# Whole vector operations in the recurrent scan, with TensorE's output and value products spread over the steps of a group

## The reference

```python
q, k = x @ W_q.T, x @ W_k.T          # per head
v = x @ W_v.T
b = (q * k).sum(-1) * SCALE
alpha = x @ W_alpha_w.T + W_alpha_b
a = -softplus(alpha).sum(-1)
vs, vl = sign(v), log(abs(v) + EPS)
def step(carry, inp):                # 64 steps, one after another
    ln, nm, sg = carry
    ln = stable_lse(a_t + ln, b_t)
    dec = a_t[..., None] + nm
    new = b_t[..., None] + vl_t[:, None, :]
    m = maximum(dec, new)
    ssum = sg * exp(dec - m) + vs_t * exp(new - m)
    nsg = sign(ssum)                 # 1 where 0
    nm = m + log(abs(ssum) + EPS)
    y = (nsg * exp(nm - ln[..., None])).sum(-2)
    return (ln, nm, nsg), y
y @ W_o.T
```

## Time and profile before

| what | value |
|---|---|
| median of 3 runs | 2039.79 us |
| profiled execution | 2044.84 us, its span 2042.4 us |
| mean granted TensorE clock | 0.943 of full speed |
| PE, DVE, ACT busy, share of the span | 92%, 65%, 55% |
| the scan's loop, first `s` to last new state | 1542.69 to 1811.08 us, 268.4 us |

### The profile page before, as it was taken

One profiled execution on the slowest core, in us unless ns is written; L12 is line 12 of the kernel. 1 busy time (PEld: TensorE's weight loads), 2 busy tenths in 40 slices (PEclk: granted clock), 3 DMA queues, 4 the chain that ended last, 5 costly groups with the idle time before them and its releaser, 6 DMA issues. The chain is left out here.

```text
span 2042.4 us, 31431 instructions
## 1 busy us (share of the span) xinstructions
PE 1881.7 (92%) x10506; PEld 1501.4 (74%) x10506; DVE 1333.6 (65%) x2451; ACT 1124.4 (55%) x1864; POOL 136.6 (7%) x130
## 2 busy tenths in 40 slices
PE   7989985999997599999999999999968899889998
PEld 4667875999996578787878787878746667665664
DVE  4784546999996474636363545454528898878686
ACT  5762324888885354545454444444426666656663
POOL 0001000111110110000000000000000000002221
PEclk9999976999999799999999999999987988879999
DMA  6300042453424221101010101012040000020000
GB/s 235 108 32 1 1 161 90 150 205 128 178 89 165 93 71 34 51 16 51 15 51 15 51 15 51 15 51 82 16 141 42 1 1 1 1 88 1 1 21 21
DMA packets 22750, 129.80 MB, mean 64 GB/s; under 512 B 3601, under 2 KB 3857, under 8 KB 18962
## 3 DMA queue, kind: packets, MB, share of 16 engines
q1 hardware_dynamic: 17714, 112.59, 15.0%
q0 software_dynamic: 4960, 16.26, 2.4%
HBM read 116.51 MB, written 12.32 MB: 63 GB/s over the span
## 5 line engine op out<-in xcount | busy, mean ns | idle before, releaser
L116 PE MATMUL PS<-cT,qs 128*128 128x512 f32 x1152 | 298.4, 404 | 3.3 <-DVE qs L1697 2.2
L116 PE MATMUL PS<-pT,cN 128*128 128x512 f32 x1152 | 269.8, 392 | 1.7 <-DVE pT L1697 1.7
L116 PEld LDWEIGHTS PS<-cT,qs 128*128 128x128 f32 x1152 | 209.5, 188 | 52.6 <-issue 8.9
L116 PEld LDWEIGHTS PS<-pT,cN 128*128 128x128 f32 x1152 | 213.9, 188 | 45.0 <-DVE pT L1697 1.9
L116 PE MATMUL PS<-fw,xgT 128*128 128x384 f32 x1104 | 204.6, 340 | 5.7 <-DVE xgT L1244 5.7
L116 PEld LDWEIGHTS PS<-fw,xgT 128*128 128x128 f32 x1104 | 193.3, 190 | 9.3 <-DVE xgT L1244 6.3
L1692 DVE TENSOR_REDUCE nmax<-PS 128x1 f32<-128x512 f32 x128 | 87.8, 686 | 156.5 <-PE PS L116 156.4
L1244 DVE TENSOR_TENSOR fw<-W,fw 128x1536 fp32r<-128x1536 f32 x92 | 159.4, 1755 | 22.8 <-ACT fw L1164 22.8
L116 PE MATMUL PS<-xT,ws 128*128 128x512 f32 x576 | 155.1, 422 | 15.1 <-PEq L2599 8.7
L1597 ACT ACTIVATE qp<-PS 128x512 f32<-128x512 f32 x96 | 57.4, 598 | 187.9 <-PE PS L116 187.9
L1164 ACT ACTIVATE fw<-W 128x1536 fp32r x92 | 134.4, 1488 | 33.2 <-issue 33.2
(11 more groups left out here) (289 smaller groups left out, 3406.8 us busy)
## 6 DMA issues: line engine op xcount, KB each, us to landing
W<-in_fc SPq DMA_DIRECT2D x8, 3072.0 KB, 11.0
cT<-in_ctxT SPq DMA_DIRECT2D x16, 768.0 KB, 4.3
raw_pj<-in_proj SPq DMA_DIRECT2D x8, 1536.0 KB
ct_in<-in_ctxT SPq DMA_DIRECT2D x16, 768.0 KB, 4.3
cn_in<-in_ctxN SPq DMA_DIRECT2D x16, 768.0 KB
W<-in_w SPq DMA_DIRECT2D x2, 4096.0 KB, 13.1
routed_y<-y POOLq DMA_DIRECT2D x22, 256.0 KB
W<-in_w SPq DMA_DIRECT2D x5, 1024.0 KB, 7.1
```

The lines of the kernel that those rows point to most:

```text
L116: mm = nc.tensor.matmul(out, lhs(m, s), rhs(n, s), start=(opens and (s, m, n) == terms[0]), stop=((s, m, n) == terms[-1]))
```

## The change

Three edits of VectorE's program, two of TensorE's, and a PSUM bank.

- `s`, `ep` and `sg` become one operation each of 512 columns. The last one, the new state, stays in halves, with ScalarE's `ear` and TensorE's `head_sums` that read it.
- eal and ebe of a group come from one operation over a tile that holds al and be side by side.
- `out_proj(c - 1)`, four steps of contraction, is spread: two of them at j = 3, one at 4, one at 5. The product for v of group c + 2 is spread: half of its 12 matmuls at j = 6, half at 7.
- The transposes of x use PSUM bank 0 in place of bank 3, so `turn_x` waits for `q_sb` in place of `z_used`, and `out_proj` no longer waits for `xT_ready`.

```diff
+    OUT_AT = {3: range(0, 2), 4: range(2, 3), 5: range(3, DK)}
...
+        coefs, small = sbuf("coefs5", [P, 2, S]), sbuf("small5", [P, 2, S])
+        (al, be), (eal, ebe) = ([tile[:, n, :] for n in range(2)] for tile in (coefs, small))
...
-        ln = Norm(nc, e, "5", sbuf, ps[3], xT[0])
+        ln = Norm(nc, e, "5", sbuf, ps[0], xT[0])
...
-                def project(c, w):
+                def project(c, w, ks=range(DK)):
...
-                    split_product(nc, bank, lambda part, k: xT[c % 2][part][:, k, :],
-                                  lambda part, k: ws[part][:, ORDER.index(w), k, :], DK, w != W5_A).then_inc(done, 1)
+                    n = ORDER.index(w)
+                    for k in ks:
+                        for m, r in ((0, 0), (0, 1), (1, 0)):
+                            mm = nc.tensor.matmul(bank, xT[c % 2][m][:, k, :], ws[r][:, n, k, :],
+                                                  start=(k == 0 and m == r and w != W5_A),
+                                                  stop=(k == DK - 1 and m == 1))
+                    if ks[-1] == DK - 1:
+                        mm.then_inc(done, 1)
...
-                    pe.wait_ge(ln.xT_ready, BASE + min(c + 4, NG))
...
-                    pe.wait_ge(z_used, BASE + max(c - 3, 0))
+                    pe.wait_ge(q_sb, BASE + c)
                     ln.tensor(pe, c)
...
-                        elif j == 5 and c >= 1:
-                            out_proj(c - 1)
+                        elif j == 6 and c + 2 < NG:
+                            project(c + 2, W5_V, range(0, 2))
                         elif j == 7 and c + 2 < NG:
-                            project(c + 2, W5_V)
+                            project(c + 2, W5_V, range(2, DK))
+                        if c >= 1 and j in OUT_AT:
+                            out_proj(c - 1, OUT_AT[j])
                         head_sums(t)
...
-                    ch.link(nc.vector.tensor_scalar(eal[:, now(c)], al[:, now(c)], EPS, None, ALU.mult))
-                    ins = nc.vector.tensor_scalar(ebe[:, now(c)], be[:, now(c)], EPS, None, ALU.mult)
+                    ins = nc.vector.tensor_scalar(small[:, :, now(c)], coefs[:, :, now(c)], EPS, None, ALU.mult)
...
-                        for h, cols in enumerate(HALVES):
-                            ve.wait_ge(r_sb, BASE + 2 * t + h + 1)
-                            nc.vector.scalar_tensor_tensor(s_[:, cols], old[:, cols], al[:, t:t + 1], bv[:, t % 2, cols],
-                                                           ALU.mult, ALU.add).then_inc(s_sb, 1)
+                        ve.wait_ge(r_sb, BASE + 2 * t + 2)
+                        nc.vector.scalar_tensor_tensor(s_[:, :], old, al[:, t:t + 1], bv[:, t % 2, :],
+                                                       ALU.mult, ALU.add).then_inc(s_sb, 2)
...
-                        for h, cols in enumerate(HALVES):
-                            ve.wait_ge(ear_sb, BASE + 2 * t + h + 1)
-                            nc.vector.tensor_tensor(ep[:, cols], ear[:, cols], ebv[:, t % 2, cols],
-                                                    ALU.max).then_inc(ep_sb, 1)
+                        ve.wait_ge(ear_sb, BASE + 2 * t + 2)
+                        nc.vector.tensor_tensor(ep[:, :], ear[:, :], ebv[:, t % 2, :], ALU.max).then_inc(ep_sb, 2)
...
+                        ve.wait_ge(s_sb, BASE + 2 * t + 2)
+                        ve.wait_ge(ep_sb, BASE + 2 * t + 2)
+                        nc.vector.scalar_tensor_tensor(sg[:, :].bitcast(U32), s_[:, :].bitcast(U32), SIGN_BIT,
+                                                       ep[:, :].bitcast(U32), ALU.bitwise_and,
+                                                       ALU.bitwise_or).then_inc(sg_sb, 2)
                         ve.wait_ge(y_mm, BASE + t + 1)
                         for h, cols in enumerate(HALVES):
-                            ve.wait_ge(sg_sb, BASE + 2 * t + h + 1)
+                            ve.wait_ge(sg_sb, BASE + 2 * t + 2)
                             nc.vector.tensor_tensor(new[:, cols], s_[:, cols], sg[:, cols], ALU.add).then_inc(r_sb, 1)
```

More of the change, by code:

```diff
@@ L1832, in decayed_attention_layer @@
         mx, dn = sbuf("mx5", [P, 1 + S]), sbuf("dn5", [P, 1 + S])
-        t1, t2, eA, eB, rd, al, be, eal, ebe = (sbuf(n, [P, S]) for n in ("t15", "t25", "eA5", "eB5", "rd5", "al5", "be5",
-                                                                       "eal5", "ebe5"))
+        t1, t2, eA, eB, rd = (sbuf(n, [P, S]) for n in ("t15", "t25", "eA5", "eB5", "rd5"))
+        coefs, small = sbuf("coefs5", [P, 2, S]), sbuf("small5", [P, 2, S])
+        (al, be), (eal, ebe) = ([tile[:, n, :] for n in range(2)] for tile in (coefs, small))
         bv, ebv = sbuf("bv5", [P, 2, D]), sbuf("ebv5", [P, 2, D])
@@ L1938, in head_sums, with out_proj @@
                     mm.then_inc(y_mm, 1)
-                def out_proj(c):
+                def out_proj(c, ks=range(DK)):
                     pe.wait_ge(yT_sb, BASE + 2 + c + 1)
-                    pe.wait_ge(ln.xT_ready, BASE + min(c + 4, NG))
                     pe.wait_ge(z_used, BASE + c)
-                    for k in range(DK):
+                    for k in ks:
                         mm = nc.tensor.matmul(ps[3], yT[:, c % 2, k, :], wo[:, k, :], start=(k == 0), stop=(k == DK - 1))
-                    mm.then_inc(z_mm, 1)
+                    if ks[-1] == DK - 1:
+                        mm.then_inc(z_mm, 1)
                 def turn_x(c):
-                    pe.wait_ge(z_used, BASE + max(c - 3, 0))
+                    pe.wait_ge(q_sb, BASE + c)
                     ln.tensor(pe, c)
```

## The result

| | median us | runs |
|---|---|---|
| before | 2040.84 | 6, 2038.75 to 2043.52 |
| after | 2051.84 | 6, 2050.11 to 2058.88 |

After over before is 1.0061, with a 95% interval of 1.0042 to 1.0079: 11 us slower, more than the 0.3% (6.1 us) that a measurement tells from no change. It lies inside the range of the prediction (2031 to 2056) and 9 us above its point.

The account below looks back on a forecast made before the run. The loop was taken as bound by VectorE's instruction stream plus waits for late ScalarE and TensorE work. Terms 4.9 + 1.8 - 1.8 - 1.4 - 0.8 + 0 = +2.7 us gave 2042.5 us, own range 2037 to 2049, full range 2031 to 2056.

Parts of the forecast that it names:

- What bounds it: Scan loop: VectorE's instruction stream plus some 18 us of waits; `ep` waits if alpha's product ends under 3.1 us before VectorE is ready.
- A plain step, +0.16 us: VectorE's plain step: 2.80 us now, 0.08 more for whole operations and 0.08 for the hold at `ep`.
- The hold of `ep` for both halves of `ear`: VectorE, each plain step: a whole `ep` waits for both halves of `ear`, between 0.01 and 0.11 us, taken as 0.08.
- The sum over 64 steps, +4.9 us: VectorE's whole operations over all scan steps: 4.9 us slower, ends -16 and +12.
- the four kinds: Scan steps by VectorE pieces behind `s` or `ep`: +0.16, +0.08, +0.06, -0.02 us; 15, 21, 16 and 12 of them.
- Behind a late `ear`, +1.8 us: Step 2 of groups 0 to 6: whole `ep` waits for `ear`'s second half, 7 x 0.25 us; ends 0 and 3.4.
- k's product -1.8: VectorE's wait for k's product: nearly all of 1.9 us goes, as VectorE arrives later; ends 0 and -1.9.
- the last output product at step 7 -0.8: Last group, step 7: `add_out`'s 0.8 us wait goes, the output product being issued from step 3 on.
- the coefficients -1.4 us: VectorE, merged eal and ebe: one chained instruction less, 0.20 us in each of seven groups inside the loop.
- TensorE's spread, 0: TensorE's spread products: lead up to 1.5 us at step 0 against slow clock, taken as 0; ends -8.7 and +16.
- the second rival: TensorE's clock stays low from the hole at step 5, making alpha's products late: +16 us, 2058.5; chance 0.14.
- The rival by which a reader costs nothing: VectorE: readers start 0.61 us behind whole operations, a step takes 2.56, kernel 2022 us; chance 0.04.

Follow-up runs that it names:

- e5: Kernel before, with the bias matmul that opens alpha's product moved from step 0 to step 4 of the group ahead: 2033.15 us, ratio 0.9961.
- e8: Changed kernel with the wait for `y_mm` put ahead of `ep`, so the state has one wait: 2053.15 us, ratio 1.0061 to the kernel before.
- e3: Changed kernel, same operations, waits placed otherwise: state and `s` one wait each, `sg` two more: 2056.8 us, ratio 1.0078 to the kernel before.
- e7: e2 with the bias matmul moved from step 0 into the hole at step 5: 2028.42 us, ratio 0.9944 to the kernel before.
- e9: Changed kernel with the bias matmul moved into the hole at step 5: 2046.02 us, ratio 1.0016 to the kernel before.
- e6: e5 with eal and ebe merged into one operation, VectorE else in halves: 2032.51 us, ratio 0.9957 to the kernel before.
- e10: e7 with eal and ebe merged into one operation: 2031.9 us, ratio 0.9944 to the kernel before.
- e1: Kernel before with VectorE's edits alone, TensorE's order and PSUM bank as before: 2051.68 us, ratio 1.0049.
- e2: Kernel before with TensorE's edits and the bank alone, VectorE in halves, coefficients apart: 2050.51 us, ratio 1.0034.

## Why the prediction was right, and where not

The range and the side of the larger risk were right; the point was not. No change that can be told had a chance of 0.56, and slower, which came, had 0.27. The forecast's own range, 2037 to 2049, was missed by 3 us. That the error of the point was no larger is in part luck: the whole operations cost some 19 us where 4.9 was forecast and 12 was the most allowed for, and 6.8 us of late ears went where 0 was forecast. Two errors of opposite sign kept the sum in the range.

Of the signs named beforehand, `s` at 0.75 and no wait for k's product or the output product inside the loop came true; the plain step (3.20, not 2.9 to 3.0) and the state behind `sg` (0.80, not 0.71) did not.

- **What bounds it.** VectorE's stream and the late product for alpha: right. e5 shows the second, since it touches nothing else. One number is misread: in groups 1 and 3 to 6 of before the product for alpha ends 3.84 us ahead of the waiting `ep` of step 2, so `ep` waits as soon as the product ends less than 3.8 us before VectorE is ready, not 3.1. At 3.1 in group 3 it had already waited 0.69. After the change the distance is 4.27, the second half of `ear` included.
- **A plain step, +0.16 us.** This is the step that failed, by its size. It was +0.40. I took the gap before a reader from L2125 and L2127, 0.03 us, where the reader has one wait. `sg`, the state and `s` have two each, the one already met ahead of the late one, and their gaps are 0.13, 0.11 and 0.13. e8 shows that for the state the wait ahead makes it, 0.07 of the 0.11; for `s` e3 leaves 0.10 with one wait. The hold of `ep` for both halves of `ear` was taken at 0.08 and is about 0.02 (0.69 from `s` to `ep`, against 0.67).
- **The sum over 64 steps, +4.9 us.** By e7 and e9 the four kinds cost 0.40, 0.38, 0.19 and 0.18 (the last from step 5 of the table, and from step 7 with the merged operation's 0.20 put back). With 15, 21, 16 and 12 of them that is 6.0 + 8.0 + 3.0 + 2.2 = 19 us, some of which lies behind late ears; e9 and e7 are 15 apart in the runs, the merged coefficients included. The upper end that I gave, 12 us, was too low as well: it priced a gap of 0.03. The trace of before had readers with two waits, `vt` (L2116) and `spread` (L2139), and they too start 0.03 behind, with the late wait first; it had none with a met wait ahead of the late one, directly behind what it reads. So no row of before could have given the price.
- **Behind a late ear, +1.8 us.** Right in kind: from `s` of step 1 to `s` of step 3 groups with the least wait take 4.32 + 4.63 in e7 (groups 4 and 5) and 4.51 + 4.94 in e9, 0.50 more, where 0.37 was forecast.
- **k's product -1.8, the last output product at step 7 -0.8, the coefficients -1.4 us.** The first two waits are gone from the profile after. The third is 0.20 per group in the timeline, too small for the runs (e6, e10).
- **TensorE's spread, 0.** By e1 against the changed kernel, 0 within the intervals. The trace fits the reason given, a lead against a slow clock: TensorE waits for VectorE ahead of step 0 of group 4 now (0.66 us), and three of seven products for alpha are slow, as before. What I did not see is that the two edits meet: on halves the same spread costs 7 us (e2), since the second rival's clock comes with it, and the changed kernel escapes because VectorE's longer steps give TensorE time. The late ears fell to 8.4 us in the changed kernel and rose to 21.8 in e2. In the runs, VectorE's edits cost 15 us between e7 and e9, where little is late, and between e2 and the changed kernel only 5.5 (ratios 1.0034 and 1.0061); the rest was hidden, it seems, by waits that TensorE's lateness made anyway. I also took the slow clock to come only behind a hole, as in group 0. Two of the three slow products of before, in groups 4 and 6, follow work at full clock: ahead of group 4's the v product took 2.96 us, TensorE was busy without a pause from 1675 on at a granted clock of 1.00, and from 1684 to 1688, under the product for alpha, the clock was 0.57. The argument against the second rival, that full work had brought the clock back in every group but group 0, left this out.
- **The tail**, 0.9 us lost, was not in the prediction: with the output product moved away from them the last head sums run at 1.2 GHz.
- **The rival by which a reader costs nothing**, and the rule of the Trainium skill beside it (page "VectorE: DVE Perf Modes", section "The DRAIN you can't avoid"): the trace disagrees more than I had read. Five instructions in place of eight, each with its reader behind it, are 0.40 us slower per step.

In the profiled executions the sum comes near: +19 - 6.8 for the late ears - 1.9 - 0.8 - 1.4 is +8.1, against +6.5 for the loop. The difference may be steps that cost nothing while `ear` was late; it was not taken apart. Add 0.9 for the tail, and 2.4 less ahead of the loop: +5.1 of span. Of these 2.4 us 1.6 arise in the layers before the fifth, which the change doesn't touch, and most of the rest is a wait of 0.7 us for the tokens' DMA that only the trace of before has; they are differences of execution, not gains. The medians are 11 apart, the rest being that before was profiled above its median and the changed kernel at its lowest; what the other executions lost more was not profiled. Products for alpha that are late in one execution and not in another would do it, as the two heaps of e2 suggest, but that is not shown.

Two things stay open: why `s` starts 0.10 us behind the state with a single wait, and whether `sg` would gain as the state did, since no kernel was run with one wait on `sg` or with its late wait first.

## What to carry to other kernels

On an engine that runs a chain of short dependent operations, cutting each into two halves hides the gap before every reader; count a merge as saved fixed cost less one such gap per reader, and take that gap from a reader whose waits are as many as yours and stand in the same order, those already met ahead of the late one or behind it. When work is spread over steps, ask what the block that is broken up was doing for the engine's clock and for the work behind it, and look for a small piece on the late path that can be moved into the hole instead. If one engine's edit is tested together with another's, test each alone too: here each hid the other.

## What the runs showed of the hardware

- On VectorE a reader right behind its producer started 0.03 to 0.04 us after the end with one wait (L2127 before, the state in e8) and with two of which the late one stood first (L2116 and L2139 before), 0.11 to 0.13 with two of which it stood last (the changed kernel), and 0.23 with four, the late one third (`sg` in e3). `s` with one wait, 0.10 (e3), does not fit this; and L143 with one wait and the increment of a semaphore between that wait and itself started 0.14 after the end of L141 (before). An independent follower started 0.08 us before the end (`sg` behind L2127 before).
- Moving one matmul of a single row, 1.12 us of work, went with a change of the clock under the twelve that follow: with it in front, three of the kernel before's seven products for alpha took 4.6 us, and without it none of e5's or e6's did (2.96 each), at the same total of work. It is not enough by itself: with the output and v products spread, two of seven in e7 and e9 and one in e10 still took 4.4 to 4.5 us without it.
- The granted clock fell to 0.57 from 1684 to 1688 in the kernel before, though TensorE had been busy without a pause and at 1.00 from 1675 on; what it did last before that was head sums of 16 columns, two matmuls of `values` and the bias matmul.
